# Vision tower: embedding, mixer output and feed-forward products with 128-token tiles as the stationary operand, program unrolled

## What is computed

```
h = patches @ tok_W                                    # 768 -> 256
x = layernorm(h)
m = (x @ in_w + in_b) * (gelu(x @ w1 + b1) @ w2 + b2)  # 256 -> 1024 -> 256
y = irfft(rfft(m over the 196 tokens) * rfft(kernel))  # circular, per feature
h = h + y @ out_w + out_b
x = layernorm(h)
h = h + x @ base_W.T + base_b + shared(x) + routed(x)  # shared is folded into base
```

## Time and profile before

| | us |
|---|---|
| timed, three runs | 1343.84, 1346.04, 1346.04 (median 1346.04) |
| profiled execution, span | 1346.5 |
| TensorE busy | 1310.8 (97%), 8008 matmuls |
| VectorE, ScalarE, GpSimd busy | 943.2, 644.0, 283.0 |

### The profile page before, as it was taken

One profiled execution on the slowest core, in us unless ns is written; L12 is line 12 of the kernel. 1 busy time (PEld: TensorE's weight loads), 2 busy tenths in 40 slices (PEclk: granted clock), 3 DMA queues, 4 the chain that ended last, 5 costly groups with the idle time before them and its releaser, 6 DMA issues.

```text
span 1346.5 us, 23512 instructions
## 1 busy us (share of the span) xinstructions
PE 1310.8 (97%) x8008; PEld 1273.8 (95%) x8008; DVE 943.2 (70%) x2571; ACT 644.0 (48%) x1169; POOL 283.0 (21%) x395
## 2 busy tenths in 40 slices
PE   6899999999999999999999999999999999999986
PEld 6889999999999999999999999999999999999975
DVE  5467776677676677676677676767776667767675
ACT  4544554444554444555444555444455444455421
POOL 3322221211221211221221222120222121222000
PEclk8899999999999999999999999999999999999986
DMA  7011101111100111110111110111110111110000
GB/s 237 1 36 49 49 12 37 48 48 48 48 24 23 48 48 48 48 39 10 48 48 48 48 48 0 48 48 48 48 48 3 45 48 48 48 49 13 1 12 25
DMA packets 18203, 56.40 MB, mean 42 GB/s; under 512 B 2160, under 2 KB 13528, under 8 KB 14168
## 3 DMA queue, kind: packets, MB, share of 16 engines
q1 hardware_dynamic: 17320, 54.93, 11.8%
q10 hardware_dynamic: 816, 0.79, 0.2%
HBM read 42.87 MB, written 12.85 MB: 41 GB/s over the span
## 4 chain that ended last, share of the span: by engine, by line
PE 95%; DVE 2%; ACT 1%; issue 1%; POOL 1%; DMA 0%; POOLq 0%; DVEq 0%
PE big L954 25%; PE big L955 24%; PE big L956 24%; PE turn L1061 4%; PE turn L987 4%; PE turn L994 3%; PE turn L1045 2%; PE turn L955 1%; PE turn L954 1%; PE turn L956 1%; PE gate_ps L954 1%; PE gate_ps L1035 1%; PE gate_ps L955 1%; PE gate_ps L956 1%; PE gate_ps L1068 1%
## 5 line engine op out<-in xcount | busy, mean ns | idle before, releaser
L347 POOL TENSOR_TENSOR patches_l<-patches,patches_h 128x392 fp32r<-128x392 f32 x186 | 189.2, 1046 | 928.6 <-ACT patches_h L421 928.6
L467 ACT ACTIVATE gelu<-big,biases 128x392 f32<-128x392 f32 x256 | 149.2, 584 | 112.6 <-PE big L956 111.4
L954 PE MATMUL big<-gelu_h,w_h 128*128 128x392 f32 x512 | 180.9, 353 | 0.0
L954 PE MATMUL big<-x_h,w_h 128*128 128x392 f32 x512 | 178.1, 348 | 1.4 <-ACT gelu L467 1.4
L440 ACT ACTIVATE norm<-turn,ln_tmp 98x256 f32<-98x256 f32 x128 | 62.1, 565 | 243.3 <-DVE ln_tmp L689 243.3
L955 PE MATMUL big<-gelu_l,w_h 128*128 128x392 f32 x512 | 175.5, 343 | 0.0
L956 PE MATMUL big<-gelu_h,w_l 128*128 128x392 f32 x512 | 174.5, 341 | 0.0
L955 PE MATMUL big<-x_l,w_h 128*128 128x392 f32 x512 | 174.2, 340 | 0.0
L956 PE MATMUL big<-x_h,w_l 128*128 128x392 f32 x512 | 174.2, 340 | 0.0
L954 PE MATMUL big<-patches_h,tokw_h 128*128 128x392 f32 x384 | 136.9, 356 | 10.0 <-POOL patches_l L359 7.6
L955 PE MATMUL big<-patches_l,tokw_h 128*128 128x392 f32 x384 | 133.4, 347 | 0.0
(11 more groups left out here) (154 smaller groups left out, 2828.0 us busy)
## 6 DMA issues: line engine op xcount, KB each, us to landing
patches<-dram_xg SPq DMA_DIRECT2D x31, 1176.0 KB, 5.5
out<-result SPq DMA_DIRECT2D x32, 392.0 KB, 2.7
patches<-dram_xg SPq DMA_DIRECT2D x3, 392.0 KB, 5.0
prod<-dram_tok_w ACTq DMA_DIRECT2D x3, 256.0 KB, 6.8
gelu<-dram_w SPq DMA_DIRECT2D x1, 512.0 KB, 7.3
h_sb<-dram_w SPq DMA_DIRECT2D x1, 512.0 KB, 8.4
result<-dram_w SPq DMA_DIRECT2D x1, 384.0 KB, 6.3
x_proj<-dram_in_w SPq DMA_DIRECT2D x1, 256.0 KB, 6.7
```

The source lines that it names most:

```text
L347: pool.tensor_tensor(patches_l[:, k, :], patches[:, k, :], patches_h[:, k, :].bitcast(F32), ALU.subtract).then_inc(pool_patches_lo, 1)
L467: act.activation(gelu[:, k % 4, :], big[UP_BANK[k]][:, 0:GT], ACT.Gelu, bias=b1_bias[:, k:k + 1]).then_inc(act_gelu, 1)
L954: pe.matmul(ps, w_h, x_h, start=first, stop=False)
```

## The change

- Tokens are cut in 98 tiles of 128. A round embeds three tiles (the first two rounds three and two), `intake_tiles`. `embed`, `mixer_out`, `base_route` and `routed` take 128 columns of tokens as the stationary operand and stream 256 weight columns (base and route together 358), so the results have tokens on partitions. `h_sb` is a ring of twelve such tiles; layer norm statistics are read from these results, and `to_tokens` and `turn_route` are gone. The output is stored from `h_sb` with tokens as rows.
- `in_w`, up, down and the Fourier transforms stay as they are, with 392 tokens streamed. x1 and y are kept in rings, since 384 tokens come in and 392 are used.
- The inverse transform streams 100 columns instead of 128.
- The embedding of round i+1 runs in step i. PSUM is three rotating banks, two for transposes, three for rows.
- GpSimd takes the low parts of gelu tiles 0 to 3 and splits all weights; VectorE keeps those of tiles 4 to 7. ScalarE's `patches_hi` does six chunks in one go and waits for the whole embedding of the round before; GpSimd follows. ScalarE normalises all three tiles of x1, VectorE all of x2. h is taken over from PSUM by VectorE with the output bias (`keep_h`).
- The gate runs in one piece, with one more operation (the router bias is added there). The base bias is a row of the routed product.
- All steps are written out; there is no loop. Behind the last step the drain handles tiles in groups of three and two.

The core of the diff (lines starting with a space or + in the order lists are the new order; removed lines are left out there):

```diff
+            def gelu_lo(g, j):
+                pool.wait_ge(act_gelu_hi, 4 * g + j + 1)
+                pool.tensor_tensor(gelu_l[:, 2 * j:2 * j + 2, :], gelu[:, 2 * j:2 * j + 2, :],
+                                   gelu_h[:, 2 * j:2 * j + 2, :].bitcast(F32), ALU.subtract)\
+                    .then_inc(pool_gelu_lo, 1)
 
...
-                else:
-                    if exists(front):
-                        patches_lo(front, LATE_K)
-                    if exists(front + 1):
-                        patches_lo(front + 1, EARLY_K)
-                    if exists(mid):
-                        fold(mid)
...
+            for i in range(1, GROUPS + 1):
+                mid = i - 1
+                gelu_lo(mid, 0)
+                gelu_lo(mid, 1)
+                if i == 1:
+                    for n in ORDER[3:]:
+                        split_lo(n)
+                if i + 2 < ROUNDS:
+                    patches_lo(i + 2)
+                fold(mid)
...
-            def patches_hi(g, ks):
-                for k in ks:
-                    if k == 0:
-                        act.wait_ge(patches_in, 16 * g)
-                        act.wait_ge(pe_embed, DH * g)
+            def patches_hi(r):
+                act.wait_ge(patches_in, 16 * (r - 1))
+                act.wait_ge(pe_embed, 2 * r)
+                for k in range(KT):
                     act.activation(patches_h[:, k, :], patches[:, k, :], ACT.Copy).then_inc(act_patches_hi, 1)
 
...
             def gelu_tile(g, k):
                 act.wait_ge(pe_w1, HC * g + k + 1)
-                if k % 2 == 0:
-
-                    if k >= 4:
-                        act.wait_ge(dve_gelu_lo, 4 * g + k // 2 - 1)
-                    elif exists(g - 1):
-                        act.wait_ge(dve_gelu_lo, 4 * (g - 1) + k // 2 + 3)
-                act.activation(gelu[:, k % 4, :], big[UP_BANK[k]][:, 0:GT], ACT.Gelu,
+                if k in (0, 2) and g > 0:
+                    act.wait_ge(dve_gelu_lo, 2 * (g - 1) + k // 2 + 1)
+                elif k in (4, 6):
+                    act.wait_ge(pool_gelu_lo, 2 * g + k // 2 - 1)
+                act.activation(gelu[:, k % 4, :], bank(g + 1, UP[k])[:, 0:GT], ACT.Gelu,
...
+            for i in range(1, GROUPS + 1):
+                mid, back, tail = i - 1, i - 2, i - 3
+                if in_range(back):
                     fold_lo(back)
...
+                if in_range(tail):
+                    gate_exp(tail, rows_ps)
+                    gate(tail, rows_ps)
+                    gated_lo(tail, bank(i, TURN_GATED))
+                if in_range(back):
+                    real_products(back)
+                    imaginary_products(back)
+                if in_range(tail):
+                    finish(tail, rows_ps)
+                if in_range(back):
                     spectrum_of_y(back)
...
                 gelu_lo(mid, 2)
                 gelu_lo(mid, 3)
...
+                if in_range(back):
+                    whole_y(back)
+                    y_lo(back)
+                if i < GROUPS:
+                    stats = stats1(i + 1)
+                    keep_h(i + 1)
+                if in_range(back):
+                    add_mixer(back, rows_ps[:, 2], bank(i, OUT)[:, 0:DIM])
+                    stats = stats2(back, 1)
+                layer_norm_scales(i + 1, stats, slice(0 if i < GROUPS else 1, 2 if in_range(back) else 1), 3)
+                if in_range(back):
+                    normalise(back, norm2, 1)
                 modulate(mid, 0)
...
+                if i < GROUPS:
+                    x1_lo(i + 1)
                 modulate(mid, 1)
...
+                if in_range(back):
+                    x2_lo(back, rows_ps, x2_h, x2_l)
...
-            def embed_block(m, k):
-                return mm3(big[EMBED_BANK[m]][:, 0:GT], tokw_h[:, k, m * P:(m + 1) * P],
-                           tokw_l[:, k, m * P:(m + 1) * P], patches_h[:, k, :], patches_l[:, k, :],
+            def mm3(ps, w_h, w_l, x_h, x_l, first, last, onto_read=False):
...
+            def embed_block(ps, high, low, t, k):
+                toks = slice(t * TILE, (t + 1) * TILE)
+                return mm3(ps, high[:, k, toks], low[:, k, toks], tokw_h[:, k, :], tokw_l[:, k, :],
                            k == 0, k == KT - 1)
...
-            def to_tokens(ps, rows, signal):
-                for t in range(TILES):
-                    for m in range(DH):
-                        c = DIM * (t % 2) + m * P
-                        ins = pe.transpose(ps[0:TT, t // 2, c:c + P], rows[:, m, t * TT:(t + 1) * TT], ident[:, :])
-                    if t % 2 == 1:
-                        ins.then_inc(signal, 1)
...
+            def base_route(d, rows, hi, lo):
+                pe.wait_ge(dve_x2_lo, DH * d + DH)
+                for t in range(len(output_tiles(d))):
+                    toks = slice(t * TILE, (t + 1) * TILE)
+                    for c in range(DH):
+                        ins = mm3(rows[:, t, 0:WIDE], hi[:, c, toks], lo[:, c, toks], wide_h[:, c, :],
+                                  wide_l[:, c, :], c == 0, c == DH - 1)
                 ins.then_inc(pe_route, 1)
 
...
-            def turn_route(g):
-                pe.wait_ge(act_route, g + 1)
-                for t in range(TILES):
-                    ins = pe.transpose(gate_ps[0:TT, t * ROUTE_COLS:(t + 1) * ROUTE_COLS],
-                                       route_sb[:, t * TT:(t + 1) * TT], ident[0:ROUTE_COLS, 0:ROUTE_COLS])
-                ins.then_inc(pe_turn_route, 1)
...
+            def mixer_out(tile, ps):
+                toks = slice((tile % Y_TILES) * TILE, (tile % Y_TILES) * TILE + TILE)
                 for c in range(DH):
...
+                    ins = mm3(ps, y_h[:, c, toks], y_l[:, c, toks], outw_h[:, c, :], outw_l[:, c, :],
+                              c == 0, c == DH - 1)
+                return ins
...
+            for i in range(1, GROUPS + 1):
                 mid, back, tail = i - 1, i - 2, i - 3
...
+                if i == 1:
+                    pe.wait_ge(weight_lo, 2)
+                project(mid)
+                if in_range(back):
+                    if back == 0:
+                        pe.wait_ge(weight_lo, len(ORDER))
                     turn_fold(back)
...
+                if in_range(tail):
+                    base_route(tail, rows_ps, x2_h, x2_l)
+                if in_range(mid - 1):
+                    pe.wait_ge(dve_mod, DH * mid)
+                mlp_up(mid, 0)
+                if in_range(back):
                     dft(back)
...
+                pe.wait_ge(act_in, DH * mid + 1)
+                mlp_up(mid, 1)
+                pe.wait_ge(act_in, DH * mid + 2)
+                mlp_up(mid, 2)
+                pe.wait_ge(act_gelu, HC * mid + 1)
+                mlp_up(mid, 3)
+                pe.wait_ge(act_gelu, HC * mid + 2)
+                if in_range(tail):
+                    turn_gated(tail, bank(i, TURN_GATED))
+                pe.wait_ge(act_gelu, HC * mid + 3)
+                mlp_up(mid, 4)
+                pe.wait_ge(act_gelu, HC * mid + 4)
+                mlp_up(mid, 5)
+                if in_range(tail):
+                    pe.wait_ge(dve_gated_lo, tail + 1)
+                mlp_up(mid, 6)
+                if in_range(tail):
+                    routed(tail, rows_ps)
+                pe.wait_ge(act_gelu, HC * mid + 5)
+                mlp_up(mid, 7)
+                if in_range(tail):
+                    pe.wait_ge(dve_result, tail + 1)
+                if i == 1:
+                    pe.wait_ge(spectrum_ready, 1)
+                    pe.wait_ge(base_sum, DH)
+                if i < GROUPS:
+                    embed(i + 1, 0)
+                if in_range(back):
                     inverse_dft(back)
...
+                if i < GROUPS:
+                    embed(i + 1, 1)
+                    embed(i + 1, 2)
+                else:
                     pe.wait_ge(act_gelu, HC * mid + 7)
...
+                    mlp_down(mid, 0, range(HC))
+                pe.wait_ge(act_gelu, HC * mid + 6)
+                if in_range(back):
+                    pe.wait_ge(dve_y_lo, DH * back + DH)
+                    mixer_tiles(back, rows_ps[:, 2], bank(i, OUT)[:, 0:DIM])
                 pe.wait_ge(act_gelu, HC * mid + 7)
...
+                if i < GROUPS:
+                    mlp_down(mid, 0, range(HC))
                 pe.wait_ge(act_gelu, HC * mid + 8)
...
                 mlp_down(mid, 1, range(4))
...
+                if i < GROUPS:
+                    if i >= 2:
+                        pe.wait_ge(dve_y, DH * back + DH)
+                    pe.wait_ge(dve_h, i)
+                    turn_x1(i + 1)
+                mlp_down(mid, 1, range(4, HC))
+                if in_range(back):
+                    turn_x2(back, rows_ps, norm2)
+
```

More of the change, by code:

```diff
@@ L46 @@
 ROUTE_COLS = ROUTED + EXPERTS
+WIDE = DIM + ROUTE_COLS
 LN_EPS = 1e-5
@@ L932, in drain @@
-                gated_lo(tail)
-                x2_lo(back)
-                gate_exp(back)
```

(34 more changed lines are left out.)

1268 lines of the change are left out of this document (582 added, 686 removed).

## The result

The changed kernel takes 1433.6 us (median of 4 runs, 1432.6 to 1435.3) against 1345.2 of the kernel before (1343.8 to 1346.0), a ratio of 1.066 with an interval of 1.0645 to 1.0675. The prediction had 1351 with a range of 1300 to 1403: the side that it gave the larger chance (slower, 0.54), but 83 us too little and outside the range. The profiled execution has a span of 1430.8 us.

A forecast was written before the change was run, and what follows sets the result against it. The prediction took TensorE, busy 97%, as the bound. From the profiled 1346.5 us it took 6 for the steady steps (39.9 against 40.11 us each), then added 2 for the head and 9 for the tail: 1351, range 1300 to 1403.

The forecast's parts named there:

- TensorE's own work: Matrix products and transposes of a step: 0.120 us per 256-column product, 0.163 per 358; work falls 2.3 to 37.8 us.
- rival F: 256-column products cost what 392-column ones do, because each loads a stationary operand: 4.6 us a step, 1485 us; chance 0.07.
- The gate: VectorE's gate chain after base_route makes TensorE wait ahead of turn_gated: 0.54 us a step where there was none.
- A: Likeliest case, the sum as laid out, gate operation not shut out by GpSimd: 1351 us, own range 1325 to 1366; chance 0.36.
- B: GpSimd's gelu low part starts first and shuts out the gate's operation: another 1.65 us a step, 1399 us; chance 0.27.
- the 0.54 us: TensorE's wait per step ahead of turn_gated from the length of the gate's chain, before any collision with GpSimd.
- The layer norm: GpSimd's patches hold up VectorE's layer-norm operations after the embedding; TensorE waits 1.6 us a step ahead of turn_x1.
- Rival C: The layer norm is not held up by GpSimd: 1.6 us a step less, 1305 us; chance 0.20.
- The head: Start of the kernel, with all weight splits on GpSimd ahead of gelu's low part: +2 us, bounds -4 to +8.
- The tail: End of the kernel, where the last two groups' gates run one after the other on VectorE: +9 us, bounds +4 to +12.
- Unrolling at nothing: Writing out the loops over the steps, without branches, was costed at no gain.
- rival D: Neither gate nor layer norm reaches TensorE, 37.8 us a step: 1290 us; chance 0.10.

The follow-up runs named there:

- b3_products_first: b1 with turn_gated one up product later on TensorE, gated_hi behind gelu 4, and the four spectrum products ahead of gated_lo on VectorE: 1302.1 us.
- g1: Changed kernel with one wait more: GpSimd starts the low part of gelu tiles 0 and 1 only after the gate's last operation with two SBUF inputs: 1368.1 us.
- g2: Changed kernel with no wait added, but two copies of two elements on GpSimd ahead of the low part of gelu tiles 0 and 1: 1369.6 us.
- b1: g1 with GpSimd waiting until x2 is normalised, then doing patches' low parts in pairs with the fold of each half between them: 1308.4 us.
- l1: Changed kernel with one wait more: GpSimd starts the low parts of the patches only when the layer norm's scales are done: 1392.9 us.
- f1: Changed kernel with TensorE filling its wait ahead of turn_gated with 14 transposes into a bank overwritten next, the wait itself kept: 1416.3 us.
- gl_both: Changed kernel with both added GpSimd waits, that of g1 and that of l1, nothing else: 1339.3 us.
- u1: Kernel before the change with its loops over three steps written out, nothing else: 1343.4 us, ratio 0.999.
- b4_tail: b3_products_first with the last two groups' gates interleaved on VectorE, separate scratch, and the previous group's gated_lo ahead of the last layer norm: 1297.9 us.

## Why the prediction was wrong

**TensorE's own work: right.** 0.118 and 0.165 a product against 0.120 and 0.163; rival F is out. The work of 37.8 us a step is confirmed to within 0.15 by b3_products_first, where the matmuls wait for nobody in a steady step and the period is 37.95.

**The gate: the mechanism was right, the choice between A and B was wrong.** This is the step that failed. The prediction had worked out that GpSimd would start at B + 5.27 and the gate's operation at B + 5.37, so its own numbers said that GpSimd is first. It put B down as a rival with 0.27, and gave A, the case in which GpSimd comes second, 0.36. The trace has 5.31 and 5.41 in the step shown, and a wait of 1.94 to 1.97 us ahead of `turn_gated` in every steady step. Taking A for the likeliest left out 1.65 us a step, 48 us. g1 and g2 show the mechanism and that 0.1 us of starting order decides; the 0.54 us that would stay without the collision came out as 0.35 to 0.42 of idle time.

**The layer norm: right in kind, 0.3 us short.** TensorE restarts at E + 10.5 instead of 10.2, and its place was at E + 8.6. So the delay is 1.9 us, not 1.6 (the 1.75 in the trace counts from the end of the last product's latency). Over 29 steps that is 9 us. The experiments agree: from g1 to b1, which differ only in when and in what order GpSimd works behind the embedding, the period falls by 1.85 us. Rival C, no hold-up, is out; l1 shows that GpSimd's work makes it. That `TENSOR_SCALAR` operations are shut out too was missed. It cost nothing here beyond the three operations, which the prediction had as three too; the 0.8 us a step in l1 are GpSimd's order of work and not this.

**The clock: missing from the sum.** The prediction priced a wait at its own length. In this kernel the 1.95 us at the gate bring twelve stretches at 1.2 GHz, about 1.45 us each, 17 us by f1 against the changed kernel. What picks these twelve steps, and only two in l1, stays open. No term, rival or bound held them.

**Head and tail: right in sign, too small.** The head is +4.9 instead of +2, inside its bounds of -4 to +8; l1, gl_both and b1, with the layer norm freed, start step 3 at 103.1, 102.8 and 100.7, so the layer norm's collision in steps 1 and 2 can be what was missing. It is not shown, since f1, whose edit begins in step 3, starts that step at 109.8. The tail is +14.4 instead of +9, beyond its bound of 12. The second gate's last operation starts 8.0 us behind the first's instead of 6: its own chain takes 5.9, but before it VectorE waits 1.15 us for `gated_h` and writes `gated_l`. That is 2 of the 5 us. Where the other 3 lie was not tested; the ten kernels with the same drain take 94.4 to 99.4 us behind the last project's start, so a part of them can be scatter.

**Unrolling at nothing: right** (u1). The Trainium skill, Runtime: NRT & Kernel Launch, Instruction fetch mechanics, let one expect a gain from the branches; these runs show none in the steady steps.

The sum with what was measured: rival B's 1399, and 9 for the layer norm, 17 for the clock, 3 for the head and 5 for the tail make 1433, against 1433.6. That it meets to 1 us is partly luck: the gate, the layer norm and the clock make 74 us over A's steady steps, where the periods show 71, and the profiled execution has a span of 1430.8. The expected gain of 67 us on TensorE's steady steps was there to be had: 63 us with the period of b3. The two collisions with the clock behind them, and 19 us of head and tail, turned it into 88 us of loss. b4_tail is 47 us faster than the kernel before, at 1297.9, and no kernel here reached rival D's 1290.

## What to carry to other kernels

Where work is moved to GpSimd, write down what VectorE runs at that time and which operands it has, down to operations of a few columns, and who waits for them: here a subtraction of 1.85 us held up one of 0.18 in a chain on which TensorE waited. If two starts are computed to lie 0.1 us apart, order them by hand, and until then take the order that the numbers give as the forecast. Price a wait of TensorE at more than its length, since its clock can fall after it: here some 17 us on top of 57 us of waiting.

## What the hardware showed that was not expected

A wait of 1.95 us is followed, in 12 of 29 steps, by 3.4 us at 1.2 GHz; in l1, by the same wait, in 2 of 29. A wait of 1.75 us in the same kernel with the first one filled is followed by none. Fourteen transposes that compute nothing remove all stretches from the steady steps and cost nothing there (1416.3 against 1433.6). GpSimd's subtraction shuts out not only operations on two SBUF tensors but also `TENSOR_SCALAR` on one: 0.94 instead of 0.17 us for six columns, and 3.24 instead of 1.06 for three of 256 columns. `gated`, with one operand in PSUM, ran beside it in g1 at 0.46, as it does alone in the changed kernel.
